# A ternary row's scales multiplied by a ratio so that its first group needs no low half: 23 matmuls in place of 24

## The chip, the cores and the metric

One core of a Trainium2 chip runs the whole program in one launch. The metric is the device time of that launch in microseconds; lower is better.

## The reference

The program is one decoder layer on x of 16 x 256 x 1024 (fp32): causal self-attention with ternary weights, cross-attention to a context of the same shape, and a gated choice among eight low-rank experts, each added to x behind a layer norm. The change is in the ternary projections alone:

```
def _ternary_dequant(w):                     # w: 1024 x 1024, groups of 128 along a row
    wg = w.reshape(O, g, GROUP_SIZE)
    scale = jnp.clip(jnp.mean(jnp.abs(wg), axis=-1, keepdims=True), EPS)
    wn = wg / scale
    q = jnp.where(wn > 0.5, 1.0, jnp.where(wn < -0.5, -1.0, 0.0))
    return (q * scale).reshape(O, I)
q, k, v = (split_heads(x @ ternary(w).T) for w in (w_q, w_k, w_v))   # x is layer-normed
q, k = rope(q), rope(k)
y = softmax(causal(q k^T / 8)) v             # 16 heads of 64
x = x + y @ ternary(w_o).T
```

## The kernel before, in words

All products run in fp16 on TensorE and keep about fp32's precision by a split: each operand is stored as a high half (rounded to fp16) and a low half (what is left), and `split_product` (L58) adds three matmuls for each of the eight 128-wide tiles of the inner dimension: high x low, low x high, high x high. That is 24 matmuls for one output, of 256 columns for a query or key tile and of 512 for a value or output tile.

**Weights.** A weight tile is 128 rows of one of w_q, w_k, w_v, w_o, 32 tiles in all. `ternary` on VectorE (L855 on) sums absolute values per group, makes the scale times 256 (`scaleW`), its fp16 rounding (`high`), thresholds, and `low` = scaleW - high, then compares twice and subtracts to get signs of -1, 0, 1. `scaled_rows` on ScalarE multiplies the signs by the scale, rounding to fp16 (8 activations of 128 columns), and by the low scale (8 more), and a DMA transpose brings the rows into `wT`. The first eight tiles come ahead of the loop, the others two or three to a step in steps 0 to 9. The factor 256 is taken out where results leave PSUM (`1.0 / W_SCALE`).

**The loop of the first half.** There are 16 batches x 8 pairs of heads = 128 pairs and 132 steps g. Each engine runs its own instruction stream in the order of the same loop and waits for the others by semaphores. In step g TensorE does, in this order: queries and keys of pair g (two products of 256 columns into one bank); scores of pair g-1; probabilities times values of pair g-2; and one product of values or of the output projection (512 columns), listed in `extra`. With s = g mod 8 the extra is: output tiles at s = 0, 1, 4, 5 and value tiles at s = 2, 3, 6, 7. What leaves PSUM goes this way:

- `projection` (ScalarE, L752): queries and keys of pair g to `raw`. A DMA (`swap`) brings the halves of each head crosswise to `swp`.
- `rotated` (VectorE, L948 to L958): in the next step raw times cosines, plus swp times sines (`sines`, GpSimd, L812), then qk's high half (L956) and low half (L958). The latter releases the scores.
- `maxima` (VectorE, L87) of both heads, `probabilities` (ScalarE, L93, L94, L762), `low_probabilities` (GpSimd, L825), a DMA transpose, and the weighted sums in the step after.
- Value tiles: `high_values` on ScalarE (L737), `low_values` on VectorE (L916). Output tiles: `add_projection` on VectorE (L933), one operation that scales and adds to x.
- Layer norms are spread over the steps: `tile_stats` and `norm_apply` (VectorE, L897 to L909), `reciprocal_root` (GpSimd, L795), `high_tile` (ScalarE, L730), `low_tile` (GpSimd, L808). The low tiles stand in steps with s = 2, 3, 5, 7, between the low probabilities of that step and the sines of the next.

In step g VectorE's order is: ternary of the step's first tile (if any), rotated of pair g-1, the value or output tile of step g-1, norm_apply, tile_stats, the second ternary, maxima of pair g-1, the weighted sum of pair g-2 (`normalised`), the third ternary. Below, "loop s" is an engine's work of a step with g mod 8 = s, and pair 8b + s is "pair s" of its block. The five banks for products are handed out in turn; a bank is free when raw is copied, or when `low_values` or `add_projection` is done.

The second half (L1010 on) runs cross-attention and experts for all batches. It computes the last four output tiles in pieces between other work, and adds them (`add_projection`, L1611).

Of the kernel before, what the change touches and what calls it, by code (L numbers as in the profile page):

```python
# [7 lines left out]
F32 = mybir.dt.float32  # L8
# [30 lines left out]


# [17 lines left out]
def split_product(pe, out, lhs, rhs, n_tiles, part=None):  # L58

    for a in part or range(n_tiles):  # L60
        for k, (i, j) in enumerate(((0, 1), (1, 0), (0, 0))):
            last = pe.matmul(out, lhs(i, a), rhs(j, a), start=a == 0 and k == 0,  # L62
                             stop=a == n_tiles - 1 and k == 2)
    return last

# [42 lines left out]
def program(nc, x, ctx, w_q, w_k, w_v, w_o, A, B, Wr, br, rope_cos, rope_sin, out):  # L108
    scratch = nc.dram_tensor("after_self_attention", (NB, T, D), F32, kind="Internal").ap()


    queries = nc.dram_tensor("queries", (NB, NT, P, 2 * D), F16, kind="Internal").ap()

    with ExitStack() as st:
# [11 lines left out]
        with ExitStack() as tmp:  # L126
# [7 lines left out]
                              scratch, queries, A, B, Wr, br, ctx, begun, yT_last)  # L134
# [15 lines left out]
def self_attention(nc, consts, banks, mats, rope_cos, rope_sin, x, scratch, queries, A, B, Wr, br,  # L150
                   ctx, begun, yT_last):
# [12 lines left out]
    wqT, wkT, wvT = [sb(f"wT{m}", [P, 2, DT, D], F16) for m in range(3)]  # L164
    xT = sb("xT", [P, 2, 2, DT, T], F16)
    v = sb("v", [P, 2, NT, H, HD + 1], F16)
    cos = sb("cos", [P, T])
    sin = sb("sin", [P, T])
    xh = sb("xh", [P, 2, D], F16)
# [3 lines left out]
    swp = sb("swp", [P, 2, T])  # L173
# [7 lines left out]
    mv = sb("mv", [P, 2])  # L181
    rstd = sb("rstd", [P, 1])
    nothing = sb("nothing", [P, 1])
    minus_half = sb("minus_half", [P, 1])
    NS = 4
    asum = sb("asum", [P, NS, NG])
    scaleW = sb("scaleW", [P, NS, NG])
    high = sb("high", [P, NS, NG], F16)
# [6 lines left out]
    def staging(name, slots, pairs):  # L195
        with ExitStack() as tmp:
            return [tmp.enter_context(nc.sbuf_tensor(f"{n}_{name}", shape, dt)) for n, shape, dt in
                    (("stage", [P, slots, D], F32), ("below", [P, D], F16),
                     ("sign", [P, pairs, D], F16), ("rows", [P, pairs, 2, D], F16))]

    first_set = staging("qkv", NS, 2)
    woT = sb("wT3", [P, 2, DT, D], F16)
# [4 lines left out]
    xin = sb("xin", [P, D])  # L207
    wT = (wqT, wkT, wvT, woT)
# [108 lines left out]
    with st:  # L317
# [8 lines left out]
        low_done = sem("low_done")  # L326
# [102 lines left out]
        def _(sp):  # L429
# [28 lines left out]
            def transpose_weights(n):  # L458
# [7 lines left out]
                to = wT[m][:, :, :, bass.ts(t, P)]  # L466
                if n < NQKV:
                    sp.wait_ge(halved, 2 * n + 2)
                    sp.dma_start_transpose(to.rearrange("p i a o -> p (i a) o"),
                                           staged(n)[3].rearrange("p i d -> p (i d)")) \  # L470
                        .then_inc(weights_transposed(n)[0], 16)
                else:
                    for i in range(2):
                        sp.wait_ge(halved, 2 * n + i + 1)
                        sp.dma_start_transpose(to[:, i], staged(n)[3][:, i]) \
                            .then_inc(half_transposed(n, i)[0], 16)

# [73 lines left out]
            for n in range(len(made[-1])):  # L551
# [4 lines left out]
                transpose_weights(n)  # L556
            for g in range(GEND):
# [19 lines left out]
                for n in tiles_at(g, 0):  # L577
                    transpose_weights(n)
                if 0 <= g - SCORES < GP:
                    transpose_probabilities(g - SCORES)  # L580
                for n in tiles_at(g, 1) + tiles_at(g, 2):
# [8 lines left out]
        def _(pe):  # L590
# [5 lines left out]
            def queries_and_keys(g):  # L596
# [7 lines left out]
                split_product(pe, to[:, 0:T], lambda i, a: wqT[:, i, a, bass.ts(s, P)],  # L604
                              lambda i, a: xT[:, b % 2, i, a, :], DT)
                split_product(pe, to[:, T:2 * T], lambda i, a: wkT[:, i, a, bass.ts(s, P)],
                              lambda i, a: xT[:, b % 2, i, a, :], DT).then_inc(j_ready, 1)
# [21 lines left out]
            def product_of_values(c):  # L629
# [6 lines left out]
                split_product(pe, to[:], lambda i, a: xT[:, b % 2, i, a, bass.ts(j // 2, P)],  # L636
                              lambda i, a: wvT[:, i, a, bass.ts(j % 2, BANK)], DT) \
                    .then_inc(j_ready, 1)

            def out_projection(c):  # L640
# [6 lines left out]
                split_product(pe, to[:], lambda i, a: yT[:, i, a, bass.ts(j // 2, P)],  # L647
                              lambda i, a: woT[:, i, a, bass.ts(j % 2, BANK)], DT) \
# [31 lines left out]
            pe.wait_ge(zeroed, 3)  # L680
# [17 lines left out]
        def _(act):  # L698
            def scaled_rows(n):
                sign, rows = staged(n)[2:]  # L700
                act.wait_ge(signs, n + 1)
                act.wait_ge(low_done, n + 1)
                if 1 < n < NQKV:
                    act.wait_ge(*weights_transposed(n - 2))
                for i, scale in ((0, scaleW), (1, low)):
                    if n > NQKV:
                        act.wait_ge(*half_transposed(n - 1, i))
                    for g in range(NG):
                        cols = bass.ts(g, GROUP)
                        last = act.activation(rows[:, i, cols], sign[:, cols], ACT.Copy,  # L710
# [21 lines left out]
            def high_values(c):  # L732
                b, j = c[1], c[2]
                act.wait_ge(j_ready, ready(c))
                if b > 0:
# [3 lines left out]
                               ACT.Copy, scale=1.0 / W_SCALE).then_inc(v_hi, 1)  # L739
# [29 lines left out]
            for g in range(GEND):  # L769
                if g - 1 in extra and extra[g - 1][0] == "v":  # L770
                    high_values(extra[g - 1])
# [4 lines left out]
                for n in tiles_at(g, 0):  # L776
                    scaled_rows(n)
                if 0 <= g - SCORES < GP:
# [13 lines left out]
        def _(pool):  # L792
# [12 lines left out]

            def low_tile(c):
# [21 lines left out]

            make_identity(pool, ident, mask, consts_done)
# [3 lines left out]
            pool.wait_ge(zeroed, 3)  # L833
            for c in norms[0:3]:
                reciprocal_root(c)
                if c in splits[0:2]:
                    low_tile(c)
            pool.wait_ge(tables_in, 32)
            for g in range(GEND):
# [843 lines left out]
```

## Time and profile before

| | us |
|---|---|
| median of 3 runs | 2355.93 (2351.03 to 2356.01) |
| profiled execution | 2353.24 |
| its span, first to last instruction | 2351.5 |
| mean granted TensorE clock | 0.972 of full |
| busy: TensorE | 2132.7 (91%) |
| busy: TensorE's weight loads | 1387.7 (59%) |
| busy: VectorE | 1503.1 (64%) |
| busy: ScalarE | 1143.3 (49%) |
| busy: GpSimd | 1086.9 (46%) |

The profile names engines PE (TensorE), PEld (its weight loads), DVE (VectorE), ACT (ScalarE), POOL (GpSimd) and SP (the queue of DMA issues). Times are microseconds from the start of the span, L12 is line 12 of the kernel. A row of the windows view gives the stretch and its length, then the busy time of PE, PEld, DVE, ACT and POOL with the number of instructions, then the granted clock, the DMA share and GB/s. A row of the timeline gives start, duration, engine, line, operation, output and input, and in brackets the idle time before it and what ended it. Ends of matmuls are modelled, so a busy PE is not PE at its peak.

### The profile page before, as it was taken

What the parts mean: (1) busy time and instruction counts of PE and PEld (TensorE: products, weight loads), DVE (VectorE), ACT (ScalarE), POOL (GpSimd) and SP (SyncE); (2) the same over time, 40 slices, a digit from 0 to 9 for tenths busy, and PEclk for the clock granted to TensorE, in tenths of its full rate; (3) what the DMA queues carried; (4) which work ended last, traced back from release to release, by engine and by line L of the source; (5) the groups of instructions that cost most, each with busy time, mean ns of one, the idle gap of its engine ahead of it and who ended that gap; (6) DMA issues with size and microseconds to landing.
All of it is one profiled execution on the core that took longest, in us unless ns stands there. A gap on an engine that the chain in (4) does not pass through costs nothing. (4 is left out here: it accounts for less than half of the span.)

```text
span 2351.5 us, 52153 instructions
## 1 busy us (share of the span) xinstructions
PE 2132.7 (91%) x19912; PEld 1387.7 (59%) x19912; DVE 1503.1 (64%) x4431; ACT 1143.3 (49%) x2562; POOL 1086.9 (46%) x983
## 2 busy tenths in 40 slices
PE   1566999999999999999999999998789998989888
PEld 1344666666666666666666666665455555555544
DVE  9988555555565556555555655545577777777774
ACT  7976433333333333333333333333676766666661
POOL 1222344444444444444444444443656565655660
PEclk9777999999999999999999999999899999999999
DMA  8876555646555556566565555558877878686852
GB/s 240 194 146 156 117 139 129 145 122 155 132 129 137 143 127 148 122 144 143 123 147 136 129 138 137 121 128 221 213 178 180 193 171 205 166 203 154 193 121 68
DMA packets 741961, 358.16 MB, mean 152 GB/s; under 512 B 688200, under 2 KB 688456, under 8 KB 741712
## 3 DMA queue, kind: packets, MB, share of 16 engines
q1 hardware_dynamic: 741712, 354.82, 64.6%
q8 instruction: 159, 2.61, 0.5%
q14 instruction: 90, 0.74, 0.1%
HBM read 104.11 MB, written 49.28 MB: 65 GB/s over the span
## 5 line engine op out<-in xcount | busy, mean ns | idle before, releaser
L825 POOL TENSOR_TENSOR halves<-prob,halves 128x384 f16<-128x384 f32 x256 | 238.6, 932 | 591.0 <-ACT halves L762 591.0
L62 PE MATMUL ps_j<-xT,wT 128*128 128x256 f16 x3744 | 428.4, 275 | 50.6 <-DMA wT<-rows_qkv 50.6
L62 PEld LDWEIGHTS ps_j<-xT,wT 128*128 128x128 f16 x3744 | 369.7, 99 | 111.7 <-issue 50.6
L87 DVE CUSTOM_DVE_ANT_0 prob<-ps_s,mask 128x128 f32<-128x128 f32 (+1 forms) x1024 | 304.4, 353 | 159.7 <-PE ps_s L77 158.3
L93 ACT ACTIVATE prob<-prob,negmax 128x128 f32<-128x128 f32 x512 | 202.0, 394 | 318.7 <-DVE negmax L87 318.6
L948 DVE TENSOR_TENSOR raw<-raw,cos 128x512 f32<-128x512 f32 x128 | 134.4, 1050 | 273.3 <-DMA swp<-raw 273.3
L952 DVE TENSOR_TENSOR raw<-raw,swp 128x512 f32<-128x512 f32 x128 | 139.7, 1091 | 231.0 <-POOL swp L812 230.2
L62 PE MATMUL ps_t<-xT,wT 128*128 128x256 f16 x2400 | 270.2, 273 | 0.0
L62 PEld LDWEIGHTS ps_t<-xT,wT 128*128 128x128 f16 x2400 | 234.9, 98 | 37.8
L1448 POOL TENSOR_TENSOR halves<-prob,halves 128x768 f16<-128x768 f32 x128 | 210.6, 1645 | 92.2 <-ACT halves L1392 92.1
L94 ACT ACTIVATE prob<-prob,negmax 128x256 f32<-128x256 f32 x512 | 252.9, 494 | 0.0
L752 ACT ACTIVATE raw<-ps_j 128x512 f32<-128x512 f32 x78 | 46.4, 595 | 401.5 <-PE ps_j L62 401.5
L812 POOL TENSOR_TENSOR swp<-swp,sin 128x512 f32<-128x512 f32 x128 | 201.5, 1574 | 37.9 <-DMA swp<-raw 37.5
L62 PE MATMUL ps_j<-wT,yT 128*128 128x512 f16 x960 | 216.6, 381 | 1.7 <-DVE xres L1611 1.7
L62 PE MATMUL ps_j<-wT,xT 128*128 128x512 f16 x912 | 206.5, 384 | 0.3 <-DMA wT<-rows_qkv 0.3
L752 ACT ACTIVATE raw<-ps_t 128x512 f32<-128x512 f32 x50 | 29.8, 596 | 264.1 <-PE ps_t L62 264.1
L795 POOL TENSOR_TENSOR rstd<-rstd,minus_half 128x1 f32<-128x1 f32 x62 | 34.0, 549 | 263.4 <-DVE rstd L902 263.4
L62 PEld LDWEIGHTS ps_j<-wT,yT 128*128 128x128 f16 x960 | 91.0, 98 | 105.2 <-issue 2.3
L62 PEld LDWEIGHTS ps_j<-wT,xT 128*128 128x128 f16 x912 | 87.7, 99 | 101.7 <-issue 5.1
L62 PE MATMUL ps_t<-wT,xT 128*128 128x512 f16 x624 | 143.3, 387 | 0.0
L762 ACT ACTIVATE halves<-prob 128x384 f16<-128x384 f32 x256 | 133.8, 523 | 8.1
L62 PE MATMUL ps_t<-wT,yT 128*128 128x512 f16 x576 | 128.2, 379 | 0.0
(186 smaller groups left out, 3630.5 us busy)
## 6 DMA issues: line engine op xcount, KB each, us to landing
swp<-raw SPq DMA_DIRECT2D x512, 64.0 KB, 2.0
xin<-in_x SPq DMA_DIRECT2D x33, 512.0 KB, 4.3
kv_ahead<-in_ctx SPq DMA_DIRECT2D x16, 1024.0 KB, 5.6
x_kept<-after_self_attention SPq DMA_DIRECT2D x16, 1024.0 KB, 5.7
xres<-in_x SPq DMA_DIRECT2D x31, 512.0 KB, 4.3
after_self_attention<-xres SPq DMA_DIRECT2D x30, 512.0 KB, 3.3
queries<-q2T SPq DMA_DIRECT2D x30, 512.0 KB, 3.0
out<-x SPq DMA_DIRECT2D x10, 1024.0 KB, 4.7
```

What stands on the lines that cost most here:

```text
L62: last = pe.matmul(out, lhs(i, a), rhs(j, a), start=a == 0 and k == 0, stop=a == n_tiles - 1 and k == 2)
L87: dve.tensor_tensor_reduce(scores[:, cols], bank[:, cols], hidden, scale, NO_SCORE, ALU.add, ALU.min, least[:, n:n + 1]).then_inc(done, 1)
L93: act.activation(prob[:, 0:P], prob[:, 0:P], ACT.Exp, scale=-1.0, bias=least[:, 0:1])
L94: return act.activation(prob[:, P:3 * P], prob[:, P:3 * P], ACT.Exp, scale=-1.0, bias=least[:, 1:2])
L752: act.activation(raw[:, g % 2].rearrange("p w n -> p (w n)"), bank(("qk", g, 0))[:], ACT.Copy, scale=1.0 / W_SCALE).then_inc(raw_done, 1)
L762: act.activation(halves[:, e, 0, :], prob[:, e], ACT.Copy) \
L795: pool.tensor_tensor(rstd[:], rstd[:], minus_half[:], ALU.pow).then_inc(ln_pow, 1)
L812: pool.tensor_tensor(swp[:], swp[:], sin[:].unsqueeze(1).broadcast_to([P, 2, T]), ALU.mult) \
L825: pool.tensor_tensor(halves[:, e, 1, :], prob[:, e], halves[:, e, 0, :], ALU.subtract).then_inc(prob_lo, 1)
L948: dve.tensor_tensor(z, z, cos[:].unsqueeze(1).broadcast_to([P, 2, T]), ALU.mult) \
L952: dve.tensor_tensor(z, z, swp[:], ALU.add).then_inc(rot_done, 1)
L1448: pool.tensor_tensor(halves[:, g % 2, :, 1, :], prob[:, g % 2], halves[:, g % 2, :, 0, :], ALU.subtract).then_inc(prob_lo, 1)
```

## The change

Each row of a weight matrix gets a ratio: the first group's scale (times 256), rounded to fp16, over the scale itself. All eight scales of the row are multiplied by it. The first group's scale then is exactly an fp16 number and has no low half, so the matmul of the first inner tile with the weights' low half is left out: 23 in place of 24 for each product. The transposed weights have 15 blocks of 128 in place of 16 (`NWH`), and ScalarE makes 15 activations per tile. The result has to be multiplied by the inverse of the ratio, per output column:

- VectorE drops `high` and `low` from `ternary` and gets two reciprocals of one column: of the first scale, and of (ratio x 256) for the previous tile (`output_factor`). GpSimd gets six small operations per tile (`scales`).
- Queries and keys have their outputs on partitions: `projection` is two activations of 256 columns with a per-partition factor, in place of one of 512.
- Values and outputs have them along the columns: the factors are stored to memory and loaded as rows on all partitions (three stores, three loads on the sync queue), and VectorE multiplies the bank in place (`scaled_values`; in `add_projection` ahead of the sum, in both halves of the program). `low_values` moves behind the maxima, `high_values` behind `projection`.

```diff
-def split_product(pe, out, lhs, rhs, n_tiles, part=None):
+def split_product(pe, out, lhs, rhs, n_tiles, part=None, exact=None):
     for a in part or range(n_tiles):
-        for k, (i, j) in enumerate(((0, 1), (1, 0), (0, 0))):
+        terms = [t for t in ((0, 1), (1, 0), (0, 0)) if a > 0 or exact is None or t[exact] == 0]
+        for t in terms:
...
+            def store_factors(k):
+                m, cols, rows = factor_part(k)
+                sp.wait_ge(factor_done, number[2 + m, cols.stop - 1] + 1)
+                with nc.allow_non_contiguous_dma("one column"):
+                    sp.dma_start(factors[m, rows].rearrange("(t p) -> p t", p=P),
+                                 factor_vo[:, m, cols]).then_inc(factor_out, 16)
+            def load_factors(k):
+                m, cols, rows = factor_part(k)
+                sp.wait_ge(factor_out, 16 * (k + 1))
+                sp.dma_start(factor_rows[:, m, rows], factors[m, rows].partition_broadcast(P)) \
+                    .then_inc(factor_in, 16)
...
             def projection(g):
-                act.activation(raw[:, g % 2].rearrange("p w n -> p (w n)"), bank(("qk", g, 0))[:],
-                               ACT.Copy, scale=1.0 / W_SCALE).then_inc(raw_done, 1)
+                for w in range(2):
+                    last = act.activation(raw[:, g % 2, w], bank(("qk", g, 0))[:, bass.ts(w, T)],
+                                          ACT.Copy, scale=factor_qk[:, w, t:t + 1])
+                last.then_inc(raw_done, 1)
...
+            def scales(n):
+                u = n % NS
+                every = ratio[:, 0, u:u + 1].broadcast_to([P, NG])
+                pool.wait_ge(inverse_done, n + 1)
+                pool.tensor_tensor(high0[:, u:u + 1], scaleW[:, u, 0:1], one[:, 0:1],
+                                   ALU.mult).then_inc(scales_done, 1)
+                pool.wait_ge(scales_done, 6 * n + 1)
+                pool.tensor_tensor(ratio[:, 0, u:u + 1], high0[:, u:u + 1], inverse0[:, u:u + 1],
+                                   ALU.mult).then_inc(scales_done, 1)
+                pool.wait_ge(scales_done, 6 * n + 2)
+                pool.tensor_tensor(ratio[:, 1, u:u + 1], ratio[:, 0, u:u + 1], one[:, 1:2],
+                                   ALU.mult).then_inc(scales_done, 1)
+                for to in (scaleR, high):
+                    pool.tensor_tensor(to[:, u, :], scaleW[:, u, :], every,
+                                       ALU.mult).then_inc(scales_done, 1)
+                pool.wait_ge(scales_done, 6 * n + 5)
+                pool.tensor_tensor(low[:, u, :], scaleR[:, u, :], high[:, u, :],
+                                   ALU.subtract).then_inc(scales_done, 1)
...
+            def output_factor(n):
+                m, t = tiles[n]
+                to = factor_qk[:, m] if m < 2 else factor_vo[:, m - 2]
+                dve.wait_ge(scales_done, 6 * n + 3)
+                dve.reciprocal(to[:, t:t + 1], ratio[:, 1, n % NS:n % NS + 1]) \
+                    .then_inc(factor_done, 1)
...
+            def scaled_values(c):
+                half = c[2] % 2
+                dve.wait_ge(j_ready, ready(c))
+                dve.wait_ge(factor_in, 16 * (half + 1))
+                dve.tensor_tensor(bank(c)[:], bank(c)[:], factor_rows[:, 0, bass.ts(half, BANK)],
+                                  ALU.mult).then_inc(v_scaled, 1)
...
             def add_projection(c):
+                dve.tensor_tensor(bank(c)[:], bank(c)[:],
+                                  factor_rows[:, 1, bass.ts(c[2] % 2, BANK)], ALU.mult) \
+                    .then_inc(out_scaled, 1)
                 dve.wait_ge(*sum_loaded(m))
-                dve.scalar_tensor_tensor(z, bank(c)[:], 1.0 / W_SCALE, z, ALU.mult, ALU.add) \
-                    .then_inc(freed(c)[0], 1)
+                dve.wait_ge(out_scaled, 4 * c[1] + c[2] + 1)
+                dve.tensor_tensor(z, bank(c)[:], z, ALU.add).then_inc(freed(c)[0], 1)
...
                 if g - 1 in extra and extra[g - 1][0] == "v":
-                    low_values(extra[g - 1])
+                    scaled_values(extra[g - 1])
...
                 if 0 <= g - SCORES < GP:
                     maxima(g - SCORES)
+                if g - 1 in extra and extra[g - 1][0] == "v":
+                    low_values(extra[g - 1])
```

## Rows read from the trace of the kernel before

**Rows 1.** Windows by stage: from:to, length, busy (instructions), granted clock, DMA share, GB/s.

```profile
58.00:212.00 154.00, 95.80 (x721) 63.41 (x718) 139.22 (x286) 122.23 (x384) 38.61 (x31) 0.80 0.78 166
275.00:1619.00 1344.00, 1343.70 (x11740) 907.93 (x11740) 773.43 (x2056) 481.09 (x1032) 622.55 (x571) 1.00 0.58 136
1619.00:2351.00 732.00, 642.59 (x7052) 379.96 (x7045) 497.03 (x1888) 463.98 (x917) 397.24 (x347) 0.97 0.73 173
```

**Rows 2.** Timeline, the copy to raw of pairs 12 and 127: start, us, engine, line.

```profile
275.18 0.60 ACT L752 ACTIVATE raw<-ps_j 128x512 f32<-128x512 f32 x1 [4.34 <-PE ps_j L62]
...
1618.83 0.60 ACT L752 ACTIVATE raw<-ps_j 128x512 f32<-128x512 f32 x1 [7.50 <-PE ps_j L62]
```

**Rows 3.** Waits of TensorE's weight loads, 275 to 1619: total, times, longest us.

```profile
PEld ps_s L73 <- DVE qk L958: 2.9, 10, 0.4
```

**Rows 4.** Timeline of one block, pairs 56 to 63: scores, first maxima, qk's low half.

```profile
800.77 0.34 PE L73 MATMUL ps_s<-qk 64*128 64x128 f16 x6
...
809.26 0.69 DVE L958 TENSOR_TENSOR qk<-raw,qk 128x512 f16<-128x512 f32 x1
...
813.15 0.29 DVE L87 CUSTOM_DVE_ANT_0 prob<-ps_s,mask 128x128 f32<-128x128 f32 x1 [0.97 <-PE ps_s L77]
...
822.92 0.69 DVE L958 TENSOR_TENSOR qk<-raw,qk 128x512 f16<-128x512 f32 x1
...
824.85 0.28 DVE L87 CUSTOM_DVE_ANT_0 prob<-ps_s,mask 128x128 f32<-128x128 f32 x1
...
834.54 0.69 DVE L958 TENSOR_TENSOR qk<-raw,qk 128x512 f16<-128x512 f32 x1
...
837.43 0.29 DVE L87 CUSTOM_DVE_ANT_0 prob<-ps_s,mask 128x128 f32<-128x128 f32 x1
...
844.73 0.69 DVE L958 TENSOR_TENSOR qk<-raw,qk 128x512 f16<-128x512 f32 x1
...
848.19 0.29 DVE L87 CUSTOM_DVE_ANT_0 prob<-ps_s,mask 128x128 f32<-128x128 f32 x1 [1.45 <-PE ps_s L77]
...
857.88 0.69 DVE L958 TENSOR_TENSOR qk<-raw,qk 128x512 f16<-128x512 f32 x1
...
860.77 0.29 DVE L87 CUSTOM_DVE_ANT_0 prob<-ps_s,mask 128x128 f32<-128x128 f32 x1
...
868.53 0.69 DVE L958 TENSOR_TENSOR qk<-raw,qk 128x512 f16<-128x512 f32 x1
...
872.14 0.29 DVE L87 CUSTOM_DVE_ANT_0 prob<-ps_s,mask 128x128 f32<-128x128 f32 x1
...
881.92 0.69 DVE L958 TENSOR_TENSOR qk<-raw,qk 128x512 f16<-128x512 f32 x1
...
882.67 0.34 PE L73 MATMUL ps_s<-qk 64*128 64x128 f16 x6
```

**Rows 5.** Timeline, the same block: cosines of pair 56, GpSimd in loop 5.

```profile
805.77 0.69 DVE L948 TENSOR_TENSOR raw<-raw,cos 128x512 f32<-128x512 f32 x1 [2.47 <-DMA swp<-raw]
...
851.54 0.92 POOL L825 TENSOR_TENSOR halves<-prob,halves 128x384 f16<-128x384 f32 x1 [0.33 <-ACT halves L762]
852.49 2.50 POOL L808 TENSOR_TENSOR xh<-xin,xh 128x1024 f16<-128x1024 f32 x1
```

**Rows 6.** Chain that ended last: start, us, what.

```profile
2316.99 5.18 PE ps_j L62 x24
```

**Rows 7.** Groups of instructions by shape: count, busy us, mean ns.

```profile
L746 ACT ACTIVATE yh<-y 128x256 f16<-128x256 f32 x128 | 51.6, 403 | 2.8 <-DVE y L966 2.8
...
L1562 DVE TENSOR_TENSOR hg_kept<-ps_j,gate 128x512 f32<-128x512 f32 x18 | 12.5, 692 | 15.2 <-PE ps_j L62 13.9 <-DVE gate L1553 0.5
...
L874 DVE TENSOR_TENSOR low<-scaleW,high 128x8 f32<-128x8 f32 x32 | 8.2, 257 | 1.1
...
L1427 POOL TENSOR_TENSOR offset<-minus_mean,rstd 128x2 f32<-128x2 f32 x16 | 3.1, 194 | 1.3
```

**Rows 8.** Timeline, a comparison of the weights while GpSimd multiplies sines.

```profile
63.91 2.29 DVE L880 TENSOR_TENSOR sign_qkv<-stage_qkv,thr 128x1024 f16<-128x1024 f32 x1
```

More of the change, by code:

```diff
@@ L38 @@
 SCALE_EPS = 1e-8
+NWH = 2 * DT - 1
 def make_identity(pool, ident, mask, done):
@@ L55, with half_tile @@
 IDENT_DONE = 4
-def split_product(pe, out, lhs, rhs, n_tiles, part=None):
+def split_product(pe, out, lhs, rhs, n_tiles, part=None, exact=None):
     for a in part or range(n_tiles):
-        for k, (i, j) in enumerate(((0, 1), (1, 0), (0, 0))):
-            last = pe.matmul(out, lhs(i, a), rhs(j, a), start=a == 0 and k == 0,
-                             stop=a == n_tiles - 1 and k == 2)
-    return last
+        terms = [t for t in ((0, 1), (1, 0), (0, 0)) if a > 0 or exact is None or t[exact] == 0]
+        for t in terms:
+            last = pe.matmul(out, lhs(t[0], a), rhs(t[1], a), start=a == 0 and t is terms[0],
+                             stop=a == n_tiles - 1 and t == (0, 0))
+    return last
+def half_tile(i, a):
+    return a if i == 0 else DT + a - 1
 def causal_scores(pe, banks, q, k, done):
@@ L180, in self_attention @@
     stats = sb("stats", [P, 2, 6])
[L181 to L184, printed above, removed]
+    small = sb("small", [P, 8])
+    one, minus_half, nothing = small[:, 0:2], small[:, 2:3], small[:, 3:4]
+    rstd, mv = small[:, 4:5], small[:, 5:7]
     NS = 4
@@ L701, in scaled_rows @@
                 act.wait_ge(signs, n + 1)
-                act.wait_ge(low_done, n + 1)
+                act.wait_ge(scales_done, 6 * n + 6)
                 if 1 < n < NQKV:
                     act.wait_ge(*weights_transposed(n - 2))
-                for i, scale in ((0, scaleW), (1, low)):
+                for i, scale in ((0, scaleR), (1, low)):
                     if n > NQKV:
                         act.wait_ge(*half_transposed(n - 1, i))
-                    for g in range(NG):
-                        cols = bass.ts(g, GROUP)
-                        last = act.activation(rows[:, i, cols], sign[:, cols], ACT.Copy,
+                    for g in range(i, NG):
+                        last = act.activation(rows[:, bass.ts(half_tile(i, g), P)],
+                                              sign[:, bass.ts(g, GROUP)], ACT.Copy,
                                               scale=scale[:, n % NS, g:g + 1])
@@ L832, in _ @@
             pool.memset(v[:, 1, :, :, HD:HD + 1], 0.0).then_inc(zeroed, 1)
[L833 to L837, printed above, removed]
+            pool.wait_ge(zeroed, 5)
+            for n in range(len(made[-1])):
+                if n < NT:
+                    reciprocal_root(norms[n])
+                scales(n)
+                if n < NT:
+                    low_tile(norms[n])
+                if n == 2 * NT:
+                    reciprocal_root(norms[NT])
             pool.wait_ge(tables_in, 32)
             for g in range(GEND):
+                for n in tiles_at(g, 0):
+                    scales(n)
                 if 0 <= g - SCORES < GP:
@@ L845, in _ @@
                     reciprocal_root(stats_at[g])
+                for n in tiles_at(g, 1):
+                    scales(n)
                 if 0 <= g - SCORES < GP:
@@ L849, in _ @@
                     low_tile(split_at[g])
+                for n in tiles_at(g, 2):
+                    scales(n)
                 for n in range(NT) if g == GP + 1 else ():
@@ L872, in ternary @@
                                       factor * SCALE_EPS, ALU.mult, bound).then_inc(scaled, 1)
-                dve.wait_ge(scaled, 4 * n + 4)
-                dve.tensor_tensor(low[:, u, :], scaleW[:, u, :], high[:, u, :],
-                                  ALU.subtract).then_inc(low_done, 1)
+                dve.wait_ge(scaled, 3 * n + 1)
+                dve.reciprocal(inverse0[:, u:u + 1], scaleW[:, u, 0:1]).then_inc(inverse_done, 1)
+                if n > 0:
+                    output_factor(n - 1)
+                dve.wait_ge(scaled, 3 * n + 3)
                 before = n - 2 if n < NQKV else n - 1
@@ L998, in _ @@
                     maxima(g - SCORES)
+                if g - 1 in extra and extra[g - 1][0] == "v":
+                    low_values(extra[g - 1])
                 for c in experts.get(g, []) if g < GP + 2 else []:
```

117 lines of the change are left out of this document (79 added, 38 removed).

## The prediction, made before the changed kernel was run

> **What bounds the kernel now.** I read the stage table first [rows 1]. From 275 to 1619 us TensorE is busy for 1343.7 of 1344 us at the full granted clock, while VectorE has 773 us of work. From 58 to 212 us it is VectorE that is full (139.2 of 154 us) and TensorE is not. After 1619 us the second half runs, which the change touches in four products only. Then I read the length of a step: raw is copied for pair 12 at 275.18 and for pair 127 at 1618.83 [rows 2], so a step is 1343.65 / 115 = 11.68 us. Last, what TensorE waits for in that stage: for qk 2.9 us in all, never over 0.4 us, and nothing else that isn't its own issue [rows 3]. By this view alone every microsecond of matmul removed would be a microsecond gained. Whether that holds depends on how far ahead of TensorE the others are, so I read one block of eight steps in the timeline [rows 4].
>
> Call Xk the start of scores(k), Mk the start of the first maxima in loop k, Qk the end of qk's low half (start of L958 + 0.69). Scores start at 800.77 for pair 56 (X0), and one step apart from there: X1 812.45, X2 824.13, X3 835.81, X4 847.49, X5 859.16, X6 870.84, X7 882.67. From the rows Q1 to Q7 are 809.95, 823.61, 835.23, 845.42, 857.88+0.69 = 858.57, 869.22 and 882.61. So qk is ready before its scores by 2.50, 0.52, 0.58, 2.07, 0.59, 1.62 and 0.06 us. Four of eight have half a microsecond or none. The reader should see why: in loops 2, 3, 5 and 7 GpSimd runs a low tile (2.50 us) between the low probabilities and the sines [rows 5], and the probabilities hang on the maxima. So there is a second chain beside TensorE: maxima, exponentials, low probabilities, low tile, sines, qk, next scores.
>
> **Part by part. TensorE.** Each product loses one of 24 matmuls. 24 matmuls of 512 columns end 5.18 us later than they start [rows 6]: 0.216 us each, 0.108 for 256 columns. A step has two products of 256 and one of 512: 0.432 us less, 11.25 us in place of 11.68. Per block 3.46 us; over 115 steps (14.4 blocks) 50 us.
>
> **VectorE, outside the weights.** A value tile gets a multiplication in PSUM behind the rotation, in the place of the old low half, whose new form comes after the maxima; an output tile gets a multiplication and then, behind its semaphore, the sum. No row writes PSUM from VectorE. The nearest is hg<-ps,gate, 0.69 us for the same 512 columns out of PSUM [rows 7]. Behind a semaphore the next one adds its whole duration and a hand-over. Below, it can be no less than the 0.6 us from start to start that the pair of operations in loop 3 shows (1.24 for two, next paragraph); above I allow 0.85, a quarter on top of the row. I take 0.69 + 0.04 = 0.73, nearest to the row. The Trainium skill (VectorE: DVE Perf Modes, the section on the TRN2 errata) gives (N+151)/0.96 ns for an fp32 tensor_tensor, 691 ns here: the row agrees, and the page has no figure for an output in PSUM.
>
> What lies between Qk-1 and Mk, when VectorE is what is late: 1.24 us in loop 3 (value tile, normalisation), 2.20 in loops 4 and 6 (a tile and the statistics), 2.92 in loop 7 (all three) [rows 4]. With the extra 0.73 for output tiles: loop 2 (output and statistics) 2.93, loop 3 1.24, loop 4 2.20, loop 5 (output and normalisation) 1.97, loop 6 2.93, loop 7 2.92: together 14.19. From Mk to Qk, from the same rows: 10.46, 10.38, 7.99, 10.38, 8.45, 10.47: together 58.13. I leave these unchanged: they are times of VectorE, ACT and GpSimd that the change does not touch, and the value tile's high half moves into an idle stretch of ACT (it waits for maxima each loop).
>
> **ScalarE.** raw becomes two activations of 256. One of 512 takes 0.60 [rows 2], one of 256 0.40 [rows 7]; with overlap of starts I take 0.2 us later (0 to 0.3). It moves Q only where the swap is what is late: Q1.
>
> **The sum of a block.** With a step of 11.25, Q1 lies 2.50 - 0.43 - 0.2 = 1.87 before X1. Then VectorE adds up without slack: X7 - X1 = 14.19 + 58.13 - 1.87 + 0.06 = 70.5 us, where TensorE alone needs 6 x 11.25 = 67.5. Loop by loop TensorE now waits about 0.4 us at scores 2, 3 and 5, and 1.9 at scores 7 (there Q6 is only just in time, so VectorE reaches the maxima 2.8 us behind X6, not 1.3). The remaining two steps take 22.5. A block is 93.0 against 93.46: 3.46 off TensorE, 3.0 given back. Over 14.4 blocks: -6 us, of which each 0.1 us more per added VectorE operation takes back some 5.
>
> What else is moved: the store of a sum stands ahead of the swap on the sync queue and now waits for a later sum. In loop 6 that is about 1.4 us behind X5; a swap lands about 4.3 us after raw is there (raw done at X0 + 0.7 = 801.5, cosines at 805.77 [rows 5]), so at about 6.2 with the store's own issue, and GpSimd is free for the sines only when the low probabilities are done, 4.27 us after the maxima began (851.54 + 0.92 - 848.19), at 2.9 + 4.3 = 7.2. Covered. The factors' three stores and loads stand on the sync queue within the first 12 loops; VectorE's backlog there hides them, so 0, and without that cover about a swap's 2 to 4 us each.
>
> **The start (to 275 us).** VectorE sets the pace, so matmuls saved are worth nothing there. Six value tiles get 0.60 more each: +3.6 us. Per weight tile two small operations go (the low scales are 0.26 [rows 7]) and two one-column reciprocals of no longer a stream come: 0, within 0.1 either way, so 2 us for 20 tiles. The six small GpSimd operations per tile (0.19 each by the row of a 128x2 product [rows 7]) run beside the comparisons; ACT may start a tile up to 1 us later, which shifts the first products once and doesn't add while VectorE is full: +1. Sum +4.5 (0 to +9).
>
> **The second half.** Four matmuls of 0.216 go, four multiplications come: -0.5.
>
> Sum: -6 + 4.5 - 0.5 = -2 on the profiled execution's 2353.2 us, whose span is 2351.5 with 1.7 around it: 2351.2. The median of the runs shown lies 2.7 higher: 2353.9, a change of -0.1%.
>
> **The rivals.** 1. TensorE stays the bound: VectorE's additions fall into its idle time and do not move the maxima. For it: VectorE is only 58% busy in the stage. Against: 0.06 to 0.59 us of readiness in half the loops. Only loop 7 and the odd hand-over would cost; a block loses some 3.1: 14.4 x 3.1 = 45 off, 2310. Chance 0.16.
>
> 2. The start grows, and the sum ends slower. Its place is VectorE from 58 to 212 us, its price GpSimd's small operations. While GpSimd multiplies the sines, the comparison beside it takes 2.29 us in place of 1.22 [rows 8]. If each of three VectorE operations of a tile pays one small GpSimd operation (0.19), 32 tiles cost 18 us: 2370. It decides once a tile costs over 0.25 us. The skill (GPSIMD Engine Reference, Specifications) says that GpSimd's SBUF interfaces are shared with VectorE, with contention for VectorE instructions with two SBUF inputs; the row agrees for large operations, none shows it for small. Chance 0.12.
>
> 3. Writing PSUM is dear: 0.85 us an operation, some +0.8 a block, +12: 2366. No row excludes it. Chance 0.08.
>
> 4. The matmuls left out don't shorten the stream (another term takes their slot): only the two free steps of a block lose 0.43 x 2 x 14.4 = 12: 2366. Chance 0.04.
>
> 5. The new waits lower TensorE's clock. In the second half TensorE is idle for 89 of 732 us and the granted clock still averages 0.97 [rows 1], against 3% idle here. If the level were 1.2 GHz for one of the two free steps of each block, that step's matmuls would take up to twice as long; half of that hidden I price at 1.7 us a block, 24 in all: 2378. The skill (TensorE: Matmul & The Clock Gate, Part 1) makes half rate the default and activity what releases it, which would speak for this rival; the stage's mean clock speaks against. Chance 0.04.
>
> **How the numbers follow.** The forecast holds 0.56, with a range of its own of 2343 to 2363 (start 0 to +9, a block -0.9 to +0.2 by the bounds of raw and the multiplication). The range 2338 to 2370 leaves out rivals 1 and 5. What a measurement can tell from no change is 0.2%, 4.7 us. Faster: 0.16 + 0.22 of the forecast = 0.38. Same: 0.25 of it. Slower: 0.09 of it + 0.28 of rivals 2 to 5 = 0.37.
>
> **What would show it.** In the profile after: TensorE's busy time from 275 us on falls by 50 us but waits for qk (L958's successor) appear, some 3 us a block, most of it in one loop of eight (first scores of the eighth pair); scores 0 and 1 have none; the first step of 11.68 comes a few microseconds later. Wrong if the waits for qk stay under 1 us a block (rival 1), if the granted clock drops within the stage (5), if the multiplication in PSUM takes more than 0.75 us (3), or if pair 12's raw comes more than 10 us later than 275 (2).

## The result and the profile after

The changed kernel takes 2364.61 us (median of 5 runs, 2363.29 to 2370.68), the kernel before, run beside it, 2356.01. The ratio is 1.0052 (95% interval 1.0035 to 1.0068; the two medians alone give 1.0037): slower by some 0.5%. The forecast was 2353.9, -0.1%. The time lies in its range, but the likeliest outcome was the wrong one.

The profiled execution of the changed kernel took 2370.68 us with a span of 2368.9. From the scores of pair 127 on it has 728.0 us, the kernel before 721.6; but two kernels of this study that change nothing in that part have 718.5 and 725.3 there (b1 and b8 below), so a difference of this size says little. The reading below is of the part ahead of it.

The windows by stage of the changed kernel (columns as in [rows 1]):

```profile
0.00:58.00 58.00, 7.42 (x43) 5.53 (x44) 52.72 (x106) 39.08 (x123) 40.13 (x73) 1.00 0.86 214
58.00:212.00 154.00, 83.37 (x616) 54.38 (x613) 121.06 (x259) 105.92 (x332) 81.40 (x135) 0.75 0.78 162
275.00:1619.00 1344.00, 1302.88 (x11413) 876.69 (x11411) 854.83 (x2178) 508.04 (x1150) 614.40 (x572) 1.00 0.59 137
1619.00:2368.00 749.00, 658.79 (x7138) 389.60 (x7136) 507.67 (x1914) 467.57 (x926) 402.06 (x352) 0.96 0.72 172
```

Two lines differ from [rows 1] in a way that speaks. In 275:1619 TensorE now has 41 us of idle time, so it no longer sets every step. And in 58:212, where the forecast had VectorE full and 4 us of work added to it, VectorE does less than before (121 in place of 139 us): it waits. Something holds up its inputs.

When did scores begin? Pair 12: 286.75 us before, 310.65 after. Pair 127: 1629.87 and 1640.93. From the changed kernel's timeline (start, us, engine, line, what it waited for):

```profile
310.65 0.34 PE L82 MATMUL ps_s<-qk 64*128 64x128 f16 x6
...
1640.93 0.34 PE L82 MATMUL ps_s<-qk 64*128 64x128 f16 x6 [2.91 <-DVE qk L1074]
```

So 23.9 us are lost ahead of pair 12, and 12.8 us are gained in the 115 steps behind it: 11.57 us a step in place of 11.68, a block of eight 92.70 in place of 93.48 (mean of pairs 24 to 120). The start is where the time went.

Pair by pair the loss at the start is no slope. Compared with the kernel before, scores are 7 to 9 us late for pairs 1 to 4, 15 us for 5 to 9, 22 and 24 us for 11 and 12: three jumps of 6 to 8 us. Each comes behind one of the three stores of factors (issued at 47.80, 154.81 and 275.07). The sync queue's own timeline around the first, and then the same transpose in the kernel before:

```profile
45.99 1.76 SPq L495 DMA_TRANSPOSE wT<-rows_qkv  x1
47.80 1.23 SPq L512 DMA_DIRECT2D factors<-factor_vo  x1
49.08 0.53 SPq L481 DMA_DIRECT2D stage_qkv<-in_L_attn_w_v  x1
50.60 10.96 SPq L495 DMA_TRANSPOSE wT<-rows_qkv  x1
61.60 0.59 SPq L518 DMA_DIRECT2D factor_rows<-factors  x1
```

```profile
50.97 2.82 SPq L469 DMA_TRANSPOSE wT<-rows_qkv  x1
```

L512 stores 512 factors, one four-byte element each. The transpose issued behind it occupies the queue for 10.96 us in place of 2.82. The windows show that the DMA engines move far less meanwhile (columns as in [rows 1]; the last two are DMA share and GB/s). First the changed kernel, then the kernel before:

```profile
50.00:56.00 6.00, 5.42 (x26) 3.80 (x27) 5.93 (x11) 5.06 (x17) 4.29 (x10) 1.00 0.48 38
56.00:62.00 6.00, 6.00 (x39) 3.69 (x38) 3.97 (x10) 0.84 (x2) 3.38 (x6) 1.00 0.54 91
```

```profile
50.00:56.00 6.00, 5.37 (x31) 3.97 (x32) 5.86 (x12) 5.69 (x20) 0.00 (x0) 1.00 0.94 185
56.00:62.00 6.00, 6.00 (x38) 3.56 (x37) 5.90 (x11) 3.90 (x13) 0.00 (x0) 1.00 0.89 188
```

38 GB/s against 185, with the engines still busy for 0.48 of the time: not only a queue that waits, but transfers that crawl. The third store does the same to the transpose of x behind it (11.89 us; 4.64 in the kernel before) and so to the swap that stands next, which goes out at 288.46:

```profile
275.07 0.59 SPq L512 DMA_DIRECT2D factors<-factor_vo  x1
275.70 0.66 SPq L523 DMA_DIRECT2D xin<-in_x  x1
276.47 11.89 SPq L537 DMA_TRANSPOSE xT<-xh  x1
288.46 3.00 SPq L572 DMA_DIRECT2D swp<-raw  x4
```

### The profile page after: what moved, and what is told of

Same layout as the page of the kernel before. It is cut to its first block and busy times, and to the rows that moved or that the text cites. A ratio compares the mean times of both kernels' runs of the same rounds, so it can differ in the third digit from the quotient of the medians.

```text
span 2368.9 us, 51963 instructions
## 1 busy us (share of the span) xinstructions
PE 2092.6 (88%) x19528; PEld 1354.3 (57%) x19528; DVE 1579.1 (67%) x4559; ACT 1163.2 (49%) x2658; POOL 1168.8 (49%) x1177
## 5 line engine op out<-in xcount | busy, mean ns | idle before, releaser
L66 PE MATMUL ps_j<-xT,wT 128*128 128x256 f16 x3588 | 414.8, 277 | 58.5 <-DMA wT<-rows_qkv 58.5
L66 PEld LDWEIGHTS ps_j<-xT,wT 128*128 128x128 f16 x3588 | 355.9, 99 | 120.2 <-issue 59.4
L813 ACT ACTIVATE raw<-ps_j,factor_qk 128x256 f32<-128x256 f32 x156 | 65.3, 469 | 415.1 <-PE ps_j L66 415.1
L66 PE MATMUL ps_t<-xT,wT 128*128 128x256 f16 x2300 | 259.2, 273 | 0.0
L66 PEld LDWEIGHTS ps_t<-xT,wT 128*128 128x128 f16 x2300 | 225.1, 98 | 36.7
L898 POOL TENSOR_TENSOR swp<-swp,sin 128x512 f32<-128x512 f32 x128 | 191.4, 1495 | 22.8 <-DMA swp<-raw 22.7
L813 ACT ACTIVATE raw<-ps_t,factor_qk 128x256 f32<-128x256 f32 x100 | 41.9, 470 | 274.3 <-PE ps_t L66 274.3
L857 POOL TENSOR_TENSOR small<-small 128x1 f32<-128x1 f32 x62 | 34.1, 550 | 274.3 <-DVE small L1008 274.3
L82 PE MATMUL ps_s<-qk 64*128 64x128 f16 x768 | 45.0, 225 | 113.3 <-DVE qk L1074 112.9
L66 PE MATMUL ps_t<-wT,xT 128*128 128x512 f16 x598 | 134.7, 382 | 0.0
```

The costliest lines, as they stand in the source:

```text
L66: last = pe.matmul(out, lhs(t[0], a), rhs(t[1], a), start=a == 0 and t is terms[0], stop=a == n_tiles - 1 and t == (0, 0))
L82: pe.matmul(banks[e][:, 0:P], q(i, rows[e], 0), k(j, rows[e])[:, 0:P], start=(i, j) == (0, 1), stop=(i, j) == (0, 0))
L813: last = act.activation(raw[:, g % 2, w], bank(("qk", g, 0))[:, bass.ts(w, T)], ACT.Copy, scale=factor_qk[:, w, t:t + 1])
L898: pool.tensor_tensor(swp[:], swp[:], sin[:].unsqueeze(1).broadcast_to([P, 2, T]), ALU.mult) \
```

## The experiments

All were timed beside the kernel before, whose median then was 2353.6 to 2354.6. "Pair 12" is the start of its scores, "block" the mean of eight steps over pairs 24 to 120, both from the profile; before has 286.75 and 93.48, the changed kernel 310.65 and 92.70.

### Is it the stores? e1 and b1

e1, on the changed kernel (VectorE reads the rows as "q (p t) -> q t p" instead):

```
-   sp.dma_start(factors[m, rows].rearrange("(t p) -> p t", p=P), ...)
+   sp.dma_start(factors[m, rows].rearrange("(p t) -> p t", p=P), ...)
```

> The changed kernel with one thing different: each partition writes its 4 or 8 factors as one run of 16 or 32 bytes, and VectorE reads the loaded factors in the order that this gives; every operation and wait is still there. Theory A (the three stores of 512, 512 and 1024 single four-byte elements hold up the sync queue's transfers behind them, 7 to 8 us each): scores of pair 12 begin near 290 us in place of 310.65, and the whole takes about 2364.6 - 20 = 2345 us. Theory B (the start is lost to GpSimd's scale operations and its longer chain before each weight tile's row copies): pair 12 stays within 3 us of 310 and the time within 3 us of 2364.

b1, on the kernel before:

```
+   pool.memset(factor_vo[:], 1.0)
+   # sync queue, behind weight tile 5, in loops 4 and 10:
+   sp.dma_start(factors[m, rows].rearrange("(t p) -> p t", p=P), factor_vo[:, m, cols])
```

> The kernel before with nothing of the change but the three stores of single four-byte elements (a constant is stored, at the places where the changed kernel stores its factors; nothing loads it). Theory A: 15 to 23 us slower than before, so 2371 to 2379, all of it before the scores of pair 12 (286.75 before, then 303 to 309). Theory B: 2356, no change.

Measured: e1 2386.67 us (ratio 1.0142, 1.0122 to 1.0161), pair 12 at 290.16, block 95.45. b1 2365.38 (1.0056, 1.0038 to 1.0074), pair 12 at 301.41, block 93.45. Theory A's account of the start holds in the main: with the stores in runs of 16 and 32 bytes, 20.5 of the 23.9 us are gone; the stores alone, in a kernel with nothing else of the change, cost 14.7 (I had put them at 16 to 22, and b1's time at 2371 to 2379). Theory B is out. But e1's total was missed by 42 us, since I had not thought of the strided operand that the other layout brings. By groups of instructions in e1, and in the changed kernel (count, busy us, mean ns):

```profile
L1055 DVE TENSOR_TENSOR ps_j<-ps_j,factor_rows 128x512 f32<-128x512 f32 x36 | 38.8, 1078 | 0.0
```

```profile
L1045 DVE TENSOR_TENSOR ps_j<-ps_j,factor_rows 128x512 f32<-128x512 f32 x36 | 24.9, 692 | 0.0
```

0.38 us more in each of the eight multiplications of a block made the block 2.75 us longer: almost one for one, as a chain that bounds the stage would have it.

### e4: runs in the store, natural order in the row

```
    # the stores as in e1
+   sp.dma_start(factor_rows[:, 1, rows] if m == 0 else raw_o, factors[m, rows]...)
+   dve.tensor_copy(factor_rows[:, m, part].rearrange("q (t p) -> q t p", p=P),
+                   (factor_rows[:, 1, part] if m == 0 else raw_o)
+                   .rearrange("q (p t) -> q t p", t=n))         # three times in all
```

> The changed kernel with each partition's factors stored as one run, as in e1, and the loaded rows put in natural order once by VectorE (three copies in all), so that the 60 later multiplications read them unit-stride as the changed kernel does. If the single-element stores cost the start and the strided operand (1.07 against 0.69 us) cost e1's steady stage, nothing else is left: scores of pair 12 at 289 to 293, block 92.7 (within 0.3), time 2343 to 2348. If e1's slower block came from something else than the stride of the operand, the block stays near 95.4 and the time near 2385.

Measured: 2345.79 us, ratio 0.9967 (0.9947 to 0.9986); pair 12 at 288.55, block 92.79. Block and time are as expected, pair 12 is 0.45 us earlier than the range. With its stores mended the change is a gain of 0.3%.

### What in a store costs? b4, b6, b7, b8

Each is b1 with one thing different (in b8 the SBUF side is cut into pairs alike).

```
b4:  n = n // 4                                    # a quarter of the elements
b6:  act.dma_start(...) in place of sp.dma_start(...)
b7:  factors[m, rows].rearrange("(p t) -> p t", p=P)        # runs of 16, 16, 32 bytes
b8:  factors[m, rows].rearrange("(a p t) -> p a t", p=P, t=2)   # elements of 8 bytes
```

> b1 with each of the three stores cut to a quarter of its elements (128, 128 and 256 in place of 512, 512 and 1024 of four bytes). If the loss goes by the number of elements: pair 12 at 289 to 293 (a quarter of 14.7 us is 3.7), time 2355 to 2359. If each store has a fixed cost: pair 12 near 301, time near 2365.

> b1 with the three stores of 512, 512 and 1024 single elements issued by ScalarE's queue in place of the sync queue, in the same loops. If what hurts is that the sync queue's own transposes and swaps stand behind the store (order within a queue): pair 12 at 286 to 290, time 2352 to 2358. If the elements hold up the DMA engines for every queue: pair 12 at 298 to 303, time 2362 to 2368.

> The twin of b1: the kernel before with the same three stores at the same places, each partition's 4, 4 and 8 values written as one run of 16, 16 and 32 bytes. If the width of an element is what costs: pair 12 at 286 to 289, time within 3 us of 2354. If any small store between the transposes costs: pair 12 at 299 or more, time 2362 to 2366.

> As b1, with elements of 8 bytes (256, 256 and 512 of them). If only four-byte elements are dear: pair 12 at 286 to 290, time 2352 to 2357. If every element in pieces, short of a partition's whole run, is dear: pair 12 at 297 to 302, time 2361 to 2366. A value between is a cost by width.

| kernel | elements | pair 12 | median us | ratio (interval) |
|---|---|---|---|---|
| b1 | 512, 512, 1024 of 4 bytes | 301.41 | 2365.38 | 1.0056 (1.0038 to 1.0074) |
| b4 | 128, 128, 256 of 4 bytes | 299.43 | 2364.37 | 1.0048 (1.0033 to 1.0063) |
| b6 | as b1, ScalarE's queue | 303.62 | 2371.93 | 1.0073 (1.0060 to 1.0085) |
| b8 | 256, 256, 512 of 8 bytes | 286.92 | 2354.60 | 1.0007 (0.9998 to 1.0015) |
| b7 | 128 runs of 16, 16, 32 bytes | 286.53 | 2352.86 | 0.9998 (0.9987 to 1.0009) |

It is the width. A quarter of the four-byte elements costs 12.7 us of the 14.7; twice as many elements of eight bytes cost nothing. Another queue does not help: behind a store issued by ScalarE a transpose of the sync queue takes 7.28 us in place of 1.75. The stores' own time from issue to landing says the same: 10.4 to 12.0 us in b6, 8.3 to 9.6 in b4, 3.6 to 4.7 in b8, 2.0 to 2.4 in b7. The windows of b1 and, below it, b8:

```profile
50.00:56.00 6.00, 5.41 (x37) 4.33 (x38) 5.87 (x12) 5.67 (x20) 0.00 (x0) 1.00 0.47 32
```

```profile
50.00:56.00 6.00, 5.26 (x25) 3.78 (x26) 5.86 (x12) 5.83 (x20) 0.00 (x0) 1.00 0.75 139
```

Of the outcomes that I had written down, the one by the number of elements (b4) and the one by the order within a queue (b6) are out; b6 came out even above its other range (303.62 and 2371.93, where I had 303 and 2368 at most). The Trainium skill (DMA: Bandwidth & Descriptors, Rules for kernel authors) says that a non-contiguous last dimension becomes one descriptor per element. The rule gives no price; if the price went by that number, b8 with its 256 and more runs would be dearer than b4 with 128 and more elements. The measurement says that here the count hardly matters. Why four bytes are so much worse than eight no run here shows.

### What bounds the steady stage? e2 and e3

```
e2:  # add_projection without (and without the wait for it)
-    dve.tensor_tensor(bank(c)[:], bank(c)[:], factor_rows[...], ALU.mult)
e3:  -  terms = [t for t in (...) if a > 0 or exact is None or t[exact] == 0]
     +  terms = [(0, 1), (1, 0), (0, 0)]
```

> The changed kernel without the in-place multiplication of the 28 output tiles of the first half by their factors (so these sums have the wrong factor, and VectorE has one operation of 0.69 us less in four loops of eight). If VectorE's chain from qk to qk bounds the steady stage, as the forecast has it, a block of eight steps falls from 92.7 to 90.6 to 91.2 us and the time by 22 to 30 us, to 2335 to 2343. If TensorE or something else bounds the stage: block within 0.4 of 92.7, time within 5 us of 2364.6.

> The changed kernel with 24 matmuls again in each product of the first half (the term that the change drops reads a high half in its place, so values differ; all scaling work of the change stays). Removed: nothing but the saving of TensorE, 0.432 us in each of 115 steps, 50 us. If VectorE's chain bounds the steady stage, most of it is hidden: block 93.2 to 94.2 in place of 92.7, time 2371 to 2386. If TensorE bounds it, the block grows by 3.4 to 96.1 and the time by 45 to 55 us, to 2410 to 2420.

Measured: e2 2350.82 us, block 91.41, so 1.29 us a block for four operations of 0.69; e3 2386.96 us, block 94.03, so 1.33 a block for matmuls worth 3.46. e3's block lies in the range of VectorE's chain (93.2 to 94.2), its time 1 us above. e2 lies between the two theories, with 14 us off in place of 22 to 30. So neither bound alone explains both. The stage has two bounds that take turns: in the changed kernel scores wait for qk in pairs 2, 3, 5 and 7 of a block only, and in e3, with TensorE slower, nearly only in pair 7 (0.5 us). The changed kernel's waits for qk from 275 to 1619 us, to be held against the 2.9 us of [rows 3]:

```profile
PEld ps_s L82 <- DVE qk L1074: 58.8, 66, 6.9
PE ps_s L82 <- DVE qk L1074: 40.7, 36, 6.6
```

### Can the other 38 us be had? e5, e6, b2, e7, b5

From loop 8 on, e5 and b2 move VectorE's sums, normalisation and statistics behind the maxima, and GpSimd's root behind the low probabilities. e6 is e4 with this order. e7 (on e6) and b5 also move GpSimd's root and low half behind the next sines, and on the sync queue the transpose of the tile behind the swap. In short:

```
     maxima(g - SCORES)
+    add_projection(extra[g - 1]) ; norm_apply(...) ; tile_stats(...)
```

> The changed kernel with VectorE's tile statistics, normalisation and output sums issued behind the maxima of their loop in place of ahead of them, from loop 8 on (GpSimd's root behind the low probabilities); the same operations. Theory: the steady stage is bound by VectorE's chain, in which only what stands between qk's low half and the maxima counts. Then the block falls from 92.7 to 89.9 (TensorE's eight steps of 11.24) to 90.8 us, and the time by 27 to 40 us to 2325 to 2338, with pair 12 still at 310. Rival: VectorE's total work or TensorE bounds the stage, its order is worth nothing: block 92.3 to 93, time 2360 to 2368.

> e4 and e5 together, a version that computes the reference and may beat both kernels. If the two losses are independent: pair 12 at 289 to 293, block 89.9 to 90.8, time 2305 to 2318. If they share a cause the gain is that of one alone, 2325 to 2345.

> The kernel before with e5's order of VectorE and GpSimd, and nothing of the change. With 24 matmuls its steady stage is bound by TensorE (0.2 to 2.4 us of slack in every step), so the order is worth nothing there: block 93.4 to 93.5, time within 4 us of 2354. If the order helped by itself, e5's gain would say nothing of the change: then 2320 to 2340.

> e6 with what e5 left in the way moved too: from loop 8 on GpSimd computes the tile's root and its low half behind the next loop's sines in place of ahead of them (0.9 and 2.1 us that stood between the low probabilities and the sines in loops 2, 3, 5, 6 and 7), and the sync queue transposes the tile behind the swap. Theory: the chain that bounds the steady stage runs over GpSimd (maxima, exponentials, low probabilities, sines, qk), so only now can TensorE set the pace: 9.1 to 9.3 us of chain against 11.24 of TensorE, block 89.9 to 90.6, pair 12 at 289 to 293, time 2306 to 2318. Rival: the wait only moves on (swap, ScalarE's raw copy): block above 91.8, time above 2333.

> The kernel before with e7's order and nothing of the change: control. TensorE's 11.68 us a step bounds it, so block 93.4 to 93.5 and time 2350 to 2357, no change beyond measurement. If it gains over 8 us, the order and not the removed matmuls is what e7 gains by.

Measured: e5 2368.13 us (block 92.66), e6 2345.21 (92.79), b2 2354.69 (93.67), e7 2388.11 (94.80), b5 2386.23 (95.33). None of the new orders gained: e5 is to be held against the changed kernel, e6 and e7 against e4's 2345.79, and e7's order cost 32 us on the kernel before as well. The maxima did begin 0.70 us behind their scores in every step of e5, as meant, but the swap was issued 2.9 and 3.0 us behind its raw at pairs 2 and 6 (mean of twelve blocks; 0.3 and 1.2 in the changed kernel). The sync queue's waits, 320 to 1560 us, show why (first the changed kernel, then e5; L550 and L552 store the sums and stand ahead of the swap):

```profile
SPq L550 <- DVE xres L1050: 17.8, 14, 3.4
```

```profile
SPq L550 <- DVE xres L1052: 82.7, 27, 5.8
```

In e7 two more things came in. Where GpSimd's low half of a tile (L898) runs beside VectorE's cast of qk (L1093), the cast takes 2.2 us (18 casts), and beside GpSimd's low half of y 0.78; in e6 all 128 take 0.43. By groups of instructions, e6 and e7:

```profile
L1089 DVE CAST qk<-raw 128x512 f16<-128x512 f32 x128 | 54.6, 427 | 4.4
```

```profile
L1093 DVE CAST qk<-raw 128x512 f16<-128x512 f32 x128 | 107.1, 837 | 4.4
```

From e7's timeline:

```profile
486.55 2.57 POOL L898 TENSOR_TENSOR xh<-xin,xh 128x1024 f16<-128x1024 f32 x1
487.18 2.23 DVE L1093 CAST qk<-raw 128x512 f16<-128x512 f32 x1
...
500.53 0.78 POOL L909 TENSOR_TENSOR yh<-y,yh 128x256 f16<-128x256 f32 x1
500.81 0.78 DVE L1093 CAST qk<-raw 128x512 f16<-128x512 f32 x1
```

The Trainium skill (GPSIMD Engine Reference, Specifications) names contention with VectorE instructions in a 2-port mode or with two SBUF inputs. The rows agree that the two engines slow each other; the cast has one input, and whether it runs in such a mode no run here shows. The other thing is the sync queue: its loads of x, which stand ahead of the swap, waited 230 us for the later low halves (51 in e6):

```profile
SPq L548 <- POOL xh L898: 117.3, 27, 5.2
SPq L525 <- POOL xh L898: 113.0, 25, 5.5
```

How the 42 us of e7 divide between the two was not tried apart.

### e9 and b9: the version that beats both

e6, with the swap ahead of the store of the sums, GpSimd's root behind the next sines and its low half left where it was:

```
-   if g in q_store: store_sum(q_store[g])
    if g < GP: swap(g)
+   if g in q_store: store_sum(q_store[g])
```

> e6 with GpSimd's root behind the next loop's sines, and on the sync queue the store of the sums behind the swap (in e5, e6 and e7 it stood ahead of the swap and waited for the sums that had been moved back; sines then began 3 us late in loops 2 and 6). GpSimd's low half of the tile stays ahead of the sines. Theory (the chain over GpSimd bounds the stage where it is longer than TensorE's 11.24): block 90.2 to 91.4, pair 12 at 289 to 293, time 2315 to 2330. Rival (another wait takes its place again): block above 92, time above 2336.

> The kernel before with e9's order, as control: TensorE's 11.68 us a step bounds it before and after, block 93.4 to 93.5, time 2350 to 2357. If it gains more than 4 us, e9's gain is not all due to the removed matmuls.

Measured: e9 2311.44 us, ratio 0.9827 (0.9814 to 0.9840), pair 12 at 290.31, block 90.12; b9 2350.30, ratio 0.9991 (0.9983 to 1.0000), block 93.42. e9 does slightly better than the theory's band (90.2 to 91.4, 2315 to 2330). The sync queue's wait for the sums falls from 80.4 us in e6 to 1.4. How much of the 34 us against e6 comes from that exchange, and how much from the moved root, was not tried apart. Eight steps of 11.24 make 89.9, so TensorE sets the pace again. Its waits for qk, 300 to 1600 us:

```profile
PEld ps_s L82 <- DVE qk L1091: 17.1, 56, 2.2
PE ps_s L82 <- DVE qk L1091: 4.2, 5, 2.0
```

The same order on the kernel before gains 3.4 us (0 to 4 by the interval). Between b9 and e9 a step falls by 0.40 us (11.675 to 11.274), 46 of the 50 us that were taken from TensorE. They had been hidden behind VectorE, GpSimd and the sync queue.

## Why the prediction was wrong

**The step that failed** stands in the paragraph on what else is moved: "The factors' three stores and loads stand on the sync queue within the first 12 loops; VectorE's backlog there hides them, so 0, and without that cover about a swap's 2 to 4 us each". They cost 22.1 us: pair 12 comes at 310.65 with single-element stores and at 288.55 in e4, which differs in the layout and three copies alone. 14.7 of that are the stores by themselves (b1). The other 7 or so go with the loads, which wait for the slow stores (the sync queue waited 6.4 us for the second). For this speaks that in b1, which loads nothing, scores are no later behind the second store than ahead of it (6.5 us at pairs 4 and 5), while the changed kernel goes from 9.3 to 15.0 there and e4 from 1.3 to 2.8. Against a clean split speaks b6, where a second store issued by ScalarE costs some 4 us without a load; the split was not tried by itself. Both halves of the step were wrong: the backlog is no cover, since it is fed by the very transposes and loads that crawl (VectorE is busy for 3.97 of the 6 us from 56 on, 5.90 before), and the price without cover was set by the swap, four transfers of 64 KB in long runs, which is not the nearest thing to 512 elements of four bytes.

**TensorE's saving**: right, 11.24 us a step where nothing waits (forecast 11.25).

**Multiplication in PSUM**: 0.69 us each, but 0.80 from start to start, which is what the sum needed and put at 0.73; read so it is past the mark of 0.75 that was set for rival 3. Its consequence, a block 0.8 us dearer, did not come (92.70), so rival 3 is out as the cause of the loss:

```profile
307.13 0.69 DVE L1045 TENSOR_TENSOR ps_j<-ps_j,factor_rows 128x512 f32<-128x512 f32 x1
307.93 0.69 DVE L1050 TENSOR_TENSOR xres<-ps_j,xres 128x512 f32<-128x512 f32 x1
```

**The block**: forecast 93.0, measured 92.70 (92.79 in e4). The places came out on the mean: over the 11.24 of TensorE the step of pair 7 has 1.5 us (forecast 1.9), those of pairs 2, 3 and 5 0.4, 0.6 and 0.2 (0.4 each), pairs 0, 1, 4 and 6 next to nothing. Pair 2's mean hides a spread: 0.1 us or less in seven of twelve blocks, 1.9 in one. The 115 steps gave 12.8 us where 6 were forecast, twice as much, since the difference of two nearly equal sums carries the error of both. Rival 1 (TensorE stays the bound) is out by e2 and e3; its 2310 had also left out the start, with which it would be some 2315. Rival 4 is out by the steps of 11.24.

**raw in two activations**: 0.84 us against 0.60, 0.24 more (0.2 taken).

**The start without the stores**: forecast +4.5, measured +1.8 in e4 and +3.4 in e1. Rival 2's sign was right, its mechanism not: the comparisons of weights take 1.22 us as before beside GpSimd's small operations (57 of 64 take 1.22 or 1.23 us, 56 before). Its sign at pair 12 (raw more than 10 us late) came true by another cause, 290.57 in place of 275.18; a sign that two mechanisms share tells neither.

**The clock**: granted at 1.00 on the mean of 275:1619, the level of 2.4 GHz, with TensorE's new idle time in it; rival 5 is out. Its price did not follow from its own terms either: half of a step of 11.25 us in each block is 5.6 us, some 80 in all, not 24.

**The sum**: put 23.9 in the place of 4.5 and -12.8 in the place of -6, and 2353.9 becomes 2366.5 (measured 2364.61). The chances (0.37 for slower) did hold the outcome, but none of their cases held the cause.

## What to carry to other kernels

Price a transfer by the nearest row in element width, not in bytes, and when none is near give it a rival of its own: here 8 KB in three stores cost 15 us, and 22 in the changed kernel, where loads wait for them. When a bound is nearly shared, removing work from one engine pays only as far as the next chain is behind, so cut that chain in the same change, and follow each moved operation to the queue that waits for it (e5 and e6 gained nothing while the swap stood behind the store of the sums; e9, with the two exchanged and the root moved, gained 34 us on e6). A control with the same order on the kernel before tells what the change itself is worth.

## What the runs showed of the hardware

- A store to DRAM in elements of four bytes holds up the DMA engines: 32 to 38 GB/s in place of 185 behind the first store, and the transposes behind the first and third stand 10.96 and 11.89 us in their queue. It does so for 128 elements nearly as much as for 512 (12.7 and 14.7 us over three stores), and from either queue (b6, 16.9 us). From issue to landing such a store takes 8.3 to 12.0 us (b4, b6), one in eight-byte elements 3.6 to 4.7 (b8), one in runs of 16 and 32 bytes 2.0 to 2.4 (b7). Eight-byte elements (0.2 us at pair 12) and the runs (none) cost scores next to nothing.
- A VectorE multiplication of 512 columns with its SBUF operand at a stride of 16 or 32 bytes takes 1.07 to 1.08 us, unit-stride 0.69. The Trainium skill (SBUF — State Buffer, Door 1: The DMA port swizzle) has a penalty for each access that crosses into a new line of 16 bytes. The trace agrees: a stride of four fp32 elements already pays, and eight pay no more. Where the page goes on to call four fp32 elements a stride that is free, e1 shows otherwise.
- GpSimd's operation on one column takes 0.19 us beside nothing and up to 1.17 us beside VectorE's comparisons, which themselves stay at 1.22 us. Beside the larger low half it is VectorE's cast that is stretched, from 0.43 to 2.23 us (e7). From the changed kernel's timeline:

```profile
37.68 1.22 DVE L986 TENSOR_TENSOR below_qkv<-stage_qkv,thr 128x1024 f16<-128x1024 f32 x1
37.78 1.17 POOL L877 TENSOR_TENSOR high<-scaleW,small 128x1 f16<-128x1 f32 x1 [0.99 <-DVE inverse L978]
...
187.13 0.19 POOL L877 TENSOR_TENSOR high<-scaleW,small 128x1 f16<-128x1 f32 x1
```
